# Cross-attention block on one core: gate, norms and query/key/value projections as one stage

## What is computed

```python
memory_proj = memory @ W_mem.T            # memory: 1601 keys x 256
attn = softmax(x @ memory_proj.T / sqrt(512))
mc = attn @ memory_proj
gate = sigmoid(concat([x, mc]) @ W_gate.T + b_gate)
x = rmsnorm(x + gate * mc, norm_w)        # first norm; the result is the residual stream
y = rmsnorm(x, ln_in_w)                   # second norm
mixed = where(vm, y @ v_qkv, y @ l_qkv)   # vm: token mask, two sets of weights ("experts")
q, k, v = split(mixed, 3); q, k = rotary(q, k)
```

## Time and profile before

| | |
|---|---|
| median of 3 runs | 3036.06 us (3020.84 to 3045.57) |
| profiled execution, its own time | 3044.3 us |
| its span, first to last instruction | 3041.3 us |
| TensorE busy / weight loads busy | 2349.0 us (77%) / 1447.3 us (48%) |
| VectorE busy | 1633.4 us (54%) |
| ScalarE busy | 944.4 us (31%) |
| GpSimd busy | 381.3 us (13%) |
| mean granted TensorE clock | 0.836 |

### The profile page before, as it was taken

The page is one execution under the profiler, slowest core; times in us unless marked ns, Lnnn a source line. Parts: engine busy times, 40 slices in busy tenths (PEclk is TensorE's granted clock), DMA queues, the critical chain, the costliest instruction groups (busy, mean ns, idle before and its releaser), DMA issues. The chain is left out here.

```text
span 3041.3 us, 32399 instructions
## 1 busy us (share of the span) xinstructions
PE 2349.0 (77%) x11966; PEld 1447.3 (48%) x11966; DVE 1633.4 (54%) x2477; ACT 944.4 (31%) x1644; POOL 381.3 (13%) x372
## 2 busy tenths in 40 slices
PE   6757858578758577775777488888888877999968
PEld 4544545354546344544544332233332315777857
DVE  3375423565442655325744377767777704766534
ACT  1211131311221212222112236756766642222101
POOL 1020002020001210020300001111111111222111
PEclk8877879787779778788868659979989958999989
DMA  2124051151161250521421724323332202333422
GB/s 82 35 84 97 15 148 51 48 131 37 64 149 35 60 122 3 121 91 35 117 65 60 129 60 93 77 39 67 65 64 48 58 10 75 91 104 104 110 76 74
DMA packets 194352, 227.67 MB, mean 75 GB/s; under 512 B 54022, under 2 KB 127626, under 8 KB 192890
## 3 DMA queue, kind: packets, MB, share of 16 engines
q1 hardware_dynamic: 187228, 217.97, 29.0%
q0 software_dynamic: 6656, 6.96, 0.9%
q10 hardware_dynamic: 288, 0.27, 0.0%
HBM read 163.28 MB, written 34.46 MB: 65 GB/s over the span
## 5 line engine op out<-in xcount | busy, mean ns | idle before, releaser
L1306 DVE TENSOR_REDUCE quarters<-ps 128x2 f32<-128x804 f32 x512 | 487.4, 989 | 174.8 <-PE ps L1340 173.8
L1262 ACT ACTIVATE pT_x<-ps 128x512 f32<-128x512 f32 (+1 forms) x832 | 451.2, 594 | 265.9 <-PE ps L1368 253.3
L164 DVE CAST w_hi<-w_raw 128x512 fp32r<-128x512 f32 (+2 forms) x365 | 209.1, 573 | 258.3 <-PE ps L172 147.7
L1368 PE MATMUL ps<-qx_ring,kx_ring 49*128 49x512 f32 (+1 forms) x832 | 233.7, 558 | 79.2 <-ACT pT_x L1262 78.6
L166 DVE TENSOR_TENSOR w_lo<-w_raw,w_hi 128x512 fp32r<-128x512 f32 (+2 forms) x365 | 257.7, 706 | 12.5
L1368 PEld LDWEIGHTS ps<-qx_ring,kx_ring 49*128 49x128 f32 (+1 forms) x832 | 85.6, 202 | 372.2 <-ACT pT_x L1262 319.0
L1381 PE MATMUL ps<-pT_x,vx_ring 128*17 128x512 f32 (+1 forms) x1664 | 259.9, 702 | 0.0
L1340 PE MATMUL ps<-kx_ring,qx_ring 48*128 48x402 f32 x1024 | 202.6, 428 | 55.9 <-DMA kx_ring<-cross_k_by_part 29.2
L170 PE MATMUL ps<-mi_h,w_hi 128*128 128x512 f32 (+1 forms) x440 | 175.1, 398 | 37.2 <-DVE w_lo L166 24.5
L754 ACT ACTIVATE pT_s<-ps 128x1024 f32<-128x1024 f32 (+3 forms) x128 | 88.1, 703 | 324.2 <-PE ps L840 324.1
L771 DVE TENSOR_REDUCE row_max_s<-ps 128x1 f32<-128x128 f32 (+3 forms) x256 | 123.9, 490 | 115.9 <-PE ps L810 111.8
(11 more groups left out here) (263 smaller groups left out, 4409.0 us busy)
## 6 DMA issues: line engine op xcount, KB each, us to landing
kx_ring<-cross_k_by_part SPq DMA_DIRECT2D x96, 200.2 KB, 7.3
w_raw<-L_xattn_l_qkv SPq DMA_DIRECT2D x48, 256.0 KB, 2.7
w_raw<-L_xattn_v_qkv SPq DMA_DIRECT2D x48, 256.0 KB, 3.1
w_raw<-L_xattn_l_gate SPq DMA_DIRECT2D x40, 256.0 KB, 2.9
w_raw<-L_xattn_l_up SPq DMA_DIRECT2D x40, 256.0 KB, 2.9
w_raw<-L_xattn_l_down SPq DMA_DIRECT2D x40, 256.0 KB, 2.7
w_raw<-w_gate_transposed SPq DMA_DIRECT2D x32, 256.0 KB, 3.0
q_st<-rhi SPq DMA_DIRECT2D x32, 256.0 KB
```

The costliest lines, as they stand in the source:

```text
L164: nc.vector.tensor_copy(hi, raw).then_inc(s_high, 1)
L1262: nc.scalar.activation(pT[0:kn, u % 3, j, :], ps[0:kn, 5 + v % 3, :], ACT.Exp, scale=SCALE)\
L1306: nc.vector.tensor_reduce(out=quarters[:, g % 2, pair, :, q, quarter], in_=ps[:, at:at + 2, 0:MAXW], axis=AX.X, op=ALU.max)\
L1368: nc.tensor.matmul(ps[0:kn, 5 + (v + par) % 3, :], k_r[rows, g % RING, pair, k0:k0 + kn], q_r[rows, g % RING, pair, :], start=True, stop=T ...
```

## The change

`gate`, `norm(1, ...)` and `qkv` become one stage, `gate_qkv`, and part of the gate goes into `memory_attention`:

- The prologue loads W_mem and the part of W_gate that acts on `mc`, multiplies them once (`w12`, 8 matmuls of 128x512 in plain float32) and stores the product in DRAM. The gate then needs 2 slabs on `cn` where it needed 4 on `mc`, and `mc` is no longer split.
- `memory_attention` loads 8 more slabs. VectorE splits the 4 slabs of W_gate for x after the mask, and the 2 of `w12` and 2 of W_mem after `cn_l`. TensorE runs the 4 x slabs of the gate (`gate_from_x`) after the last weighted sum: one before the sums of probabilities, one before the spreading of the reciprocals, two after it.
- `gate_qkv`: the 2 slabs of `w12`, the 2 of W_mem, then the projections. These take the *unnormalised* stream, times both norm weights (`w_both`) and the mask: `fuse`, `mask_x`, `rest_x` on VectorE, with ScalarE's rounded copy between the last two. Slabs go expert by expert, not alternating. The two norm factors are per token: they go into the cosine and sine tables (`cos_r`, `sin_r`) and, as a column `rs_col`, into the copy of the values. Squares are added up by GpSimd (6 additions), with one matmul with ones for each norm between the two experts of the keys; Ln, Exp and VectorE's `second_sums`, `tables` and the scaling of `h` follow in the stage.
- The memsets go; the matmuls on `q_st` and `k_st` read 96 and 97 rows instead of 128.

```diff
+                    sp.wait_ge(s_w12c, ET)
+                    sp.dma_start(w12_d.rearrange("(a p) n -> p a n", p=P), w12[:, :, :]).then_inc(s_st, 16)
...
+                    pe.wait_ge(s_wm, 32)
+                    for e in range(ET):
+                        for k in range(DT):
+                            last = nc.tensor.matmul(ps[:, 2 + e, :], wm[:, k, e * P:(e + 1) * P], wg[:, k, :],
+                                                    start=k == 0, stop=k == DT - 1)
+                        last.then_inc(s_w12, 1)
...
+                        for n, src in enumerate(after):
+                            load_w(sp, DT + n, src, wl, s["s_ws"])
...
+                        for n in range(DT, 2 * DT):
+                            split_w(dve, n, wl, s["s_wh"], s["s_ws"], s["s_wu"])
...
+                        for n in range(2 * DT, DT + len(after)):
+                            split_w(dve, n, wl, s["s_wh"], s["s_ws"], s["s_wu"])
...
+                        def gate_from_x(k):
+
+                            pe.wait_ge(s["s_ws"], DT + k + 1)
+                            for j in range(DT):
+                                cut = slice(j * P, (j + 1) * P)
+                                last = three(ps[:, GATE_BANKS[j], :], w_hi[:, k, cut], w_lo[:, k, cut], xh[:, k, :], xl[:, k, :],
+                                             k == 0, False)
+                            last.then_inc(s["s_wu"], 1)
+
+                        gate_from_x(0)
...
                         pe.wait_ge(s["s_acc"], KT)
 
                         for q in range(ST):
                             last = nc.tensor.matmul(ps[:, 7, q:q + 1], acc[:, q * P:(q + 1) * P], ones[:, 0:1],
                                                     start=True, stop=True)
                         last.then_inc(s["s_sum"], 1)
+                        gate_from_x(1)
...
+                        gate_from_x(2)
+                        gate_from_x(3)
...
+                            g, e, k = n // G, n % G // DT, n % DT
...
+                            if n == RAW - 1:
+                                sp.dma_start(k_st[STACK:STACK + 1, :, :].bitcast(f32).rearrange("a (r h) n -> a r (h n)", r=8),
+                                             ones_d[:, 0:NH // 8 * S].rearrange("(a r) n -> a r n", a=1)).then_inc(s["s_ones"], 16)
...
+                        for n in range(2):
+                            for k in range(DT):
+                                nc.scalar.activation(sq[n][:, k, :], h[:, k, :], ACT.Square,
+                                                     scale=cols[:, 0, k:k + 1] if n else 1.0).then_inc(s["s_sq"], 1)
...
+                        for n, (rs, src) in enumerate(((rs0, ps[:, bank[0], :]), (rs1, rs1[:, :]))):
+                            if n == 0:
+                                act.wait_ge(s["s_ss"], 1)
+                            else:
+                                act.wait_ge(s["s_tab"], 2)
+                            nc.scalar.activation(rs[:, :], src, ACT.Ln, bias=eps_col[:, 0:1], scale=1.0 / D).then_inc(s["s_rs"], 1)
+                            act.wait_ge(s["s_rs"], 2 * n + 1)
+                            nc.scalar.activation(rs[:, :], rs[:, :], ACT.Exp, scale=-0.5).then_inc(s["s_rs"], 1)
...
-                        nc.gpsimd.memset(q_st[3 * HD:P, :, :].bitcast(f32), 0.0).then_inc(s["s_z"], 1)
-                        pool.wait_ge(s["s_z"], 1)
-                        nc.gpsimd.memset(k_st[3 * HD:P, :, :].bitcast(f32), 0.0).then_inc(s["s_z"], 1)
...
+                        for n in range(2):
+                            for k in range(1, DT):
+                                pool.wait_ge(s["s_sq"], n * DT + k + 1)
+                                if k > 1:
+                                    pool.wait_ge(s["s_sum"], n * (DT - 1) + k - 1)
+                                nc.gpsimd.tensor_tensor(out=sq[n][:, 0, :], in0=sq[n][:, 0, :], in1=sq[n][:, k, :], op=ALU.add)\
+                                    .then_inc(s["s_sum"], 1)
...
+                        def fuse(j):
+
+                            dve.wait_ge(s["s_eg"], j + 1)
+                            dve.wait_ge(s["s_b"], j + 1)
+                            nc.vector.tensor_tensor(out=eg[:, j, :], in0=eg[:, j, :], in1=ps[:, MC_BANKS[j], :], op=ALU.mult)\
+                                .then_inc(s["s_g"], 1)
+                            dve.wait_ge(s["s_g"], 2 * j + 1)
+                            nc.vector.tensor_tensor(out=h[:, j, :], in0=eg[:, j, :], in1=xT[:, j, :], op=ALU.add)\
+                                .then_inc(s["s_g"], 1)
+
+                        def mask_x(n):
+
+                            e, k = divmod(n, DT)
+                            if n >= 2:
+                                dve.wait_ge(s["s_xl"], n - 1)
+                            if e == 0:
+                                dve.wait_ge(s["s_g"], 2 * k + 2)
+                            nc.vector.scalar_tensor_tensor(out=full[:, n % 2, :], in0=h[:, k, :], scalar=w_both[:, k:k + 1],
+                                                           in1=keep_expert[:, e, :], op0=ALU.mult, op1=ALU.mult).then_inc(s["s_x"], 1)
+
+                        def rest_x(n):
+
+                            e, k = divmod(n, DT)
+                            dve.wait_ge(s["s_xh"], n + 1)
+                            nc.vector.tensor_tensor(out=xe[e][1][:, k, :], in0=full[:, n % 2, :],
+                                                    in1=xe[e][0][:, k, :].bitcast(f32), op=ALU.subtract).then_inc(s["s_xl"], 1)
...
+                            dve.wait_ge(s["s_rs"], 2)
+                            nc.vector.tensor_tensor(out=rs1[:, :], in0=rs0[:, :], in1=rs0[:, :], op=ALU.mult).then_inc(s["s_tab"], 1)
+                            dve.wait_ge(s["s_ss"], 2)
+                            dve.wait_ge(s["s_tab"], 1)
+                            nc.vector.tensor_tensor(out=rs1[:, :], in0=rs1[:, :], in1=ps[:, bank[1], :], op=ALU.mult)\
+                                .then_inc(s["s_tab"], 1)
...
+                            dve.wait_ge(s["s_rs"], 4)
+                            nc.vector.tensor_tensor(out=rs1[:, :], in0=rs1[:, :], in1=rs0[:, :], op=ALU.mult).then_inc(s["s_tab"], 1)
+                            dve.wait_ge(s["s_tab"], 3)
+                            nc.vector.tensor_tensor(out=cos_r, in0=cos_t[:, :], in1=rs1[:, :], op=ALU.mult).then_inc(s["s_tab"], 1)
+                            nc.vector.tensor_tensor(out=sin_r, in0=sin_t[:, :], in1=rs1[:, :], op=ALU.mult).then_inc(s["s_tab"], 1)
...
+                        split(0)
+                        split(1)
+                        for j in range(DT + 1):
+                            if j < DT:
+                                fuse(j)
+                                mask_x(j)
+                            if j:
+                                rest_x(j - 1)
+                            if j in (2, 3):
+                                split(j)
+                        for n in range(DT, 2 * DT + 1):
+                            if n < 2 * DT:
+                                mask_x(n)
+                            if n > DT:
+                                rest_x(n - 1)
+                                split(n - 1)
+                        for n in range(G, G + DT):
+                            split(n)
...
+                        split(G + DT)
+                        second_sums()
+                        for n in range(G + DT + 1, 2 * G):
+                            split(n)
...
+                        tables()
+                        dve.wait_ge(s["s_sq"], 2 * DT)
+                        for k in range(DT):
+                            nc.vector.scalar_tensor_tensor(out=h[:, k, :], in0=h[:, k, :], scalar=cols[:, 0, k:k + 1],
+                                                           in1=rs0[:, :], op0=ALU.mult, op1=ALU.mult).then_inc(s["s_h"], 1)
+                        for n in range(2 * G, 2 * G + 2):
+                            split(n)
...
+                            if 2 * G + 2 + c < 3 * G:
+                                split(2 * G + 2 + c)
+                        dve.wait_ge(s["s_rc"], 1)
+                        nc.vector.tensor_copy(rs_col[:, :], ps[:, GATE_BANKS[0], 0:ST]).then_inc(s["s_rcc"], 1)
...
+                        for j in range(DT):
+                            cut = slice(j * P, (j + 1) * P)
+                            for k in range(ET):
+                                last = three(ps[:, GATE_BANKS[j], :], w_hi[:, k, cut], w_lo[:, k, cut], cn_h[:, k, :], cn_l[:, k, :],
+                                             False, k == ET - 1)
+                            last.then_inc(s["s_c"], 1)
+                        for j in range(DT):
+                            cut = slice(j * P, (j + 1) * P)
+                            for k in range(ET):
+                                last = three(ps[:, MC_BANKS[j], :], w_hi[:, ET + k, cut], w_lo[:, ET + k, cut],
```

(51 more changed lines are left out.)

225 lines of the change are left out of this document (95 added, 130 removed).

## The result

The changed kernel takes **2909.85 us**, the median of 4 runs (2904.11 to 2963.8); the kernel before, beside it on the same chip, takes 3032.4 (median of 4, 3020.84 to 3045.57). The ratio is 0.9588, 95% interval 0.9536 to 0.9641: 4.1% faster. Runs more than 1.5% above the fastest of their kernel are left out of the ratios where enough others remain: here the one at 2963.8, in E7 2912.56 and 2953.25, while E2's ratio keeps its two, 3078.12 and 3083.11. The profiled execution took 2910.25 us, 2908.0 of it span, 25 more than the 2885.1 that the prediction's sum gave for it, and lies inside the range.

What follows compares the result with a forecast made beforehand. Stages behind barriers made critical chains count in full, with no engine full in qkv. Four stretches saving 167.8 us, less 8.6 for the prologue, gave 2885.1 profiled; allowing for that execution being 8.2 above median, 2877 us, range 2840 to 2930.

Steps and rivals of the forecast that it cites:

- 1: `cn_l` ends: Memory attention's tail: `cn_l` ends at 105.3 us on batch 0's clock; next stage starts at 110.6, 9.5 later than the gate.
- 2: w12 part ends: Gate: 24 `w12` matmuls take 8.0 us at a fallen clock, to 118.6; W_mem's 24 end at 124.2.
- 3: last query slab: Mixing and queries: VectorE leads with fuse, mask, rest and splits; the last 128-wide query slab ends at 145.0 us.
- 4: first Ln: Keys: four wide slabs 11.2 us, sum with ones to 157.1, second sums to 161.2, three splits to 164.4.
- 5: rotary loop starts: Second root 4.2 us with VectorE waiting, tables 2.1, scaling of `h` 2.73, two splits 2.1: to 172.3.
- 6: first stacking DMA: Rotary loop with splits to 188.5 us, then 24 stacking DMAs, 23.3, and 3.0: to 214.8.
- the six additions of GpSimd: Squares added beside VectorE's splits: priced at nothing; 6 us a batch, 24 in all, if the splits' lead is gone.
- low clock: Rival: TensorE at half clock in the new stage, 20 us a batch, 80 in all: about 2957 us; chance 0.12.
- the norms are not hidden: Rival: squares or additions in the new stage also late (6 us), result near 2900; within the forecast's 0.75.
- the rows of the scores at nothing: Self-attention matmuls over 96 or 97 rows instead of 128: priced at nothing, between -5 and +5 us over all.
- slower: Rival: clock never lifts in gate and projections, 36 us slower than before, about 3070 us; chance 0.03.
- more gain: Rival: clock kept in step 2, uncontended rotary turns, shorter hop: 6 us a batch, 2853; chance 0.08 below 2840.

Runs made afterwards that it cites:

- E7: Changed kernel with late GpSimd additions, key splits before `second_sums`, two value splits before the tables, scaling of `h` last: 2895.19 us, ratio 0.9427 to the kernel before.
- E2: Kernel before with 96 and 97 rows in the self-attention's matmuls and the two GpSimd memsets removed: 3058.76 us, ratio 1.0108.
- E4: Changed kernel with GpSimd's six additions begun only when weight slab 11 is split: 2904.1 us, ratio 0.9571 to the kernel before.
- E5: Changed kernel with the scaling of `h` moved from ahead of the rotary loop to the end of VectorE's list: 2903.28 us, ratio 0.9556 to the kernel before.
- E6: Changed kernel with the splits of key slabs 13 to 15 ahead of `second_sums` on VectorE: 2919.16 us, ratio 0.9567 to the kernel before.
- E1: Kernel before with only the self-attention's matmuls on `q_st` and `k_st` cut from 128 to 96 and 97 rows: 3056.48 us, ratio 1.0078.
- E10: E7 with 128 rows in the self-attention's matmuls, the extra rows cleared by ScalarE as in E8: 2859.05 us, ratio 0.9421 to the kernel before.
- E11: E7 run again, with more rounds, on the same chip as E10: 2875.95 us, ratio 0.9474 to the kernel before.
- E9: Changed kernel with the self-attention's 256 maximum matmuls over 32 rows instead of 96: 2985.2 us, ratio 0.9822 to the kernel before.
- E8: Changed kernel with 128 rows again in the self-attention's matmuls, rows 96 to 127 cleared by eight ScalarE copies: 2908.95 us, ratio 0.9533 to the kernel before.

## Why the prediction was right, and where its sum was off

The direction, the mechanism and the range were right; the gain was 122.6 us between the medians measured together where 159.2 was worked out. By its steps, in us from the end of the weighted sums of batch 0:

| step | predicted | after |
|---|---|---|
| 1: `cn_l` ends; next stage's first load | 10.9; 16.2 | 10.7; 16.0 |
| 2: w12 part ends | 24.2 | 23.5 |
| 3: last query slab | 50.6 | 53.3 |
| 4: first Ln | 62.7 | 67.8 |
| 5: rotary loop starts | 77.9 | 83.8 |
| 6: first stacking DMA; first late DMA | 94.1; 120.4 | 100.0; 126.6 |

1. **Steps 1, 2, 6 and the prologue held** to within 0.7 us. The loop takes 16.2 us as forecast, the DMAs 26.6 where 26.3 was said, the prologue 8.4 where 8.6 was.
2. **Mis-sized: the six additions of GpSimd, taken at nothing.** The lead of VectorE's splits over TensorE that was to cover them didn't exist on the last query slab (TensorE waits 1.63 us) and the first key slab (0.26). E4 shows 2.4 us a batch on average, inside the bound of 6. The Trainium skill, "GPSIMD Engine Reference", section Specifications, says that GpSimd's SBUF interfaces are shared with VectorE; the trace agrees, cast 0.42 to 1.51, subtraction 0.69 to 1.65. I had the rule and its rows, and chose the low end of the range.
3. **Mis-sized in step 4: the wide key slabs.** 11.2 us at full clock were said. From the first one at 154.25 to the end of the last it was 13.4, clock 0.84: the first of them still ran at the lower level. The additions didn't bring that about: the clock fell before the wait that they caused, and in E4, without them, it fell as well and these slabs took as long. What is seen each time is narrow slabs with a gap of 0.8 us between them; what lets the clock fall there is open. This is part of the rival "low clock", in two places (here and in the narrow key slabs) and not in the whole stage. That rival's sum was too small besides: it took the short query slabs at 1.28 us each, their price at full clock, where a step of 0.21 us makes them 2.5, so that it stood for some 2977 and not 2957.
4. **Mis-sized in step 5: the scaling,** 2.73 said, 4.65 measured, beside GpSimd. Alone it is worth 1.6 (E5), since TensorE's narrow slabs end almost as late. Step 5 is only 0.8 too long in all, because the second root took 2.7 us and not 4.2: the second wait of VectorE, which the prediction named as a sign, isn't there. Steps 4 and 5 are a net of three chains: E5 and E6 show that taking out one wait uncovers the next, which a sum along a single chain, as mine was, can't show.
5. **The rival "the norms are not hidden" held in mechanism.** It put the result near 2900. But the fault was not in late squares: TensorE waits 3.15 us behind `second_sums`, its clock falls in that gap (without it, in E6, it doesn't), and with the splits first the tables wait 2.74 us for the root. With everything in order 118.3 us are reached (E7), 2 less than my sum.
6. **Failed: the rows of the scores at nothing, -5 to +5 over all.** It was +25.8 in the trace; the edit alone costs 24 us (E1), undoing it gives 17 (E10 against E11). Over all traces but E9, the 16 self-attentions with 128 rows take 123.6 us on average (116.9 to 126.1), the 36 with 96 and 97 rows 128.3 (124.2 to 133.2): 4.6 a batch, 18 in all. Single batches overlap, the means of the kernels don't: 122.6 to 124.6 in the four with 128 rows, 125.2 to 130.3 in the nine with 96 and 97. **What stays open** is why. The traces show a lower mean granted clock at equal instruction counts and equal busy time times clock, no more. Whether the clock follows the rows as such, or the edit shifted the moments at which it changes, no run separates; E9 was meant to and failed.
7. **By chance:** -4.2 ahead of the stretch and -17.4 behind all batches. Without these the result would have been some 22 us higher, about 2931, just above the range. That range was itself a little wide at the top: 10 us a batch and the prologue at 12, which is 3.4 above the 8.6 of the sum, give 2920; 2930 comes out only if the 12 are counted whole. Neither the rival "slower" nor "more gain" came: the gate's and the queries' windows have clocks of 0.77 and 0.91.

## What to carry to other kernels

Where a stage is a net of chains, work out each engine's order to the end of the stage and not one chain: take out all waits that meet at the same point, and measure them together as well as one by one. An operation moved to GpSimd because its own chain has slack was paid for by VectorE here, so give it the window in which VectorE's results are least urgent. And price a cut in a matmul's rows as a change that can go either way: here it saved the 6 us a batch that two memsets held up (E2 against E1) and cost 4 to 6 in the scores.

## What was not expected of the hardware

- 96 and 97 contraction rows in place of 128 go with a longer self-attention at the same counts: 128.3 us against 123.6 a batch, mean granted clock 0.73 to 0.75 in after against 0.77 to 0.81 in before. The reason is not shown.
- A float32 matmul of 32 rows behind a 128-row mask matmul makes the step longer, 0.71 us against 0.49: its weight load starts 0.16 us behind the load before it and not 0.01.
- Two DMAs that spread one DRAM row of zeros over 32 and 31 partitions held up the weight slabs behind them, and VectorE waited 26.95 us for the first; for most of that time one DMA engine of 16 was at work, at 26 GB/s. Four ScalarE copies that clear 32 partitions of `k_st` take 7.33 us and, where they stand, delay nothing (a stretch of 126.4 to 126.6 us in E8 against 124.8 to 126.6 in after).
